# A new order of VectorE's drains and low parts at the beginning of a block, and an earlier split of a22, in a Strassen-style adapter kernel on one core

## The reference, cut to what matters

```python
W = weights[condition]                             # 64 x 64 per batch element, one of 16
c = einsum('bct,bcd->bdt', x, W)                   # x: 64 x 64 x 1024
logits = c_flat @ gate_w.T + expert_bias           # 4 experts
one_hot = one_hot(argmax(logits))
base = einsum('bth,oh->bto', c, W_up)              # W_up: 1024 x 1024
z = einsum('nh,erh->ner', c_flat, lora_A)          # rank 8 for each expert
d = einsum('ner,ehr->neh', z, lora_B)              # ALPHA / RANK is 1
delta = einsum('neh,ne->nh', d, one_hot)           # only the chosen expert's
out = x + base + delta
```

## Time and profile before

| what | value |
|---|---|
| median of three runs | 444.32 us |
| the profiled execution's own time | 443.3 us |
| span of that execution, first to last instruction | 441.4 us |
| TensorE busy | 433.1 us (98%) |
| VectorE busy | 351.6 us (80%) |
| ScalarE busy | 198.3 us (45%) |
| GpSimd busy | 115.9 us (26%) |
| granted TensorE clock over the span | 1.000 |

### The profile page before, as it was taken

How to read it: one execution, slowest core, us unless ns; L and a number is a source line. 1 busy time by engine, 2 the same in 40 slices (tenths; PEclk the granted TensorE clock), 3 DMA queues, 4 the chain that set the end, 5 groups by cost and what they waited for, 6 DMA issues and landing times.

```text
span 441.4 us, 8929 instructions
## 1 busy us (share of the span) xinstructions
PE 433.1 (98%) x3138; PEld 410.5 (93%) x3139; DVE 351.6 (80%) x644; ACT 198.3 (45%) x310; POOL 115.9 (26%) x95
## 2 busy tenths in 40 slices
PE   7999998999999999999999999999999999999997
PEld 7889987999999999999999999999999999999996
DVE  3999879697796969789686969879696977969663
ACT  5895335263444426254543525354352624453210
POOL 3991050220505031040504013050502205050310
PEclk9999999999999999999999999999999999999999
DMA  9900032230403122130313213031222214031102
GB/s 236 404 6 1 1 120 71 75 119 25 162 28 117 50 104 86 48 143 24 119 60 106 71 48 143 24 132 58 95 71 91 99 40 151 24 119 48 73 25 97
DMA packets 17375, 38.73 MB, mean 88 GB/s; under 512 B 3854, under 2 KB 4110, under 8 KB 17362
## 3 DMA queue, kind: packets, MB, share of 16 engines
q1 hardware_dynamic: 16162, 38.02, 24.4%
q10 hardware_dynamic: 1040, 0.26, 0.3%
q0 software_dynamic: 160, 0.28, 0.2%
HBM read 21.78 MB, written 16.78 MB: 87 GB/s over the span
## 4 chain that ended last, share of the span: by engine, by line
PE 86%; DVE 7%; issue 6%; POOL 1%; ACT 0%; DVEq 0%; POOLq 0%
PE bank_y L614 25%; PE bank_x L614 24%; PE y_ps L550 11%; PE bank_c L614 10%; PE bank_b L614 9%; PE bank_x L672 2%; DVE w_s L817 2%; DVE w_a L817 1%; DVE x_hl L784 1%; PE bank_y L620 1%; PE bank_c L620 1%; PE bank_b L620 1%; PE bank_x L620 1%; PE bank_y L651 1%; DVE hl_s L794 1%
## 5 line engine op out<-in xcount | busy, mean ns | idle before, releaser
L326 POOL TENSOR_TENSOR s_sum<-a 128x512 f32<-128x512 f32 x16 | 20.7, 1294 | 294.6 <-DVE a L789 294.6
L384 ACT ACTIVATE x_hl<-x_sb 64x1024 fp32r<-64x1024 f32 x64 | 67.8, 1059 | 57.9 <-DMA x_sb<-in_x_dram 57.1
L784 DVE TENSOR_TENSOR x_hl<-x_sb,x_hl 64x1024 fp32r<-64x1024 f32 x64 | 78.2, 1221 | 8.2 <-ACT x_hl L384 6.2
L614 PE MATMUL bank_x<-w_a,hl_a 128*128 128x292 f32 (+1 forms) x576 | 76.1, 288 | 0.0
L614 PEld LDWEIGHTS bank_x<-w_a,hl_a 128*128 128x128 f32 x576 | 73.5, 189 | 0.5
L614 PE MATMUL bank_y<-w_a,hl_a 128*128 128x256 f32 (+1 forms) x552 | 72.9, 288 | 0.0
L614 PEld LDWEIGHTS bank_y<-w_a,hl_a 128*128 128x128 f32 x552 | 70.7, 189 | 0.4
L388 ACT ACTIVATE y_small<-y_ps 128x512 f32<-128x512 f32 x62 | 37.1, 598 | 74.1 <-PE y_ps L550 74.0
L550 PE MATMUL y_ps<-cond_hl,x_hl 128*128 x496 | 63.7, 271 | 2.3 <-DVE a L789 1.0
L550 PEld LDWEIGHTS y_ps<-cond_hl,x_hl 128*128 128x128 f32 x496 | 61.5, 191 | 4.7 <-DVE a L789 1.5
L789 DVE TENSOR_TENSOR a<-y_ps,y_small 128x512 f32<-128x512 f32 x62 | 42.6, 686 | 12.9 <-ACT y_small L388 12.2
(11 more groups left out here) (129 smaller groups left out, 471.5 us busy)
## 6 DMA issues: line engine op xcount, KB each, us to landing
x_sb<-in_x_dram SPq DMA_DIRECT2D x32, 512.0 KB, 3.3
out_dram<-x_sb SPq DMA_DIRECT2D x63, 256.0 KB, 2.0
w_raw<-in_L_ffn_W_up_dram SPq DMA_DIRECT2D x8, 512.0 KB, 11.3
cond_sb<-in_L_cond_weights_dram ACTq DMA_DIRECT2D x1, 256.0 KB, 5.2
cond_sb<-in_L_cond_weights_dram SPq DMA_DIRECT2D x1, 256.0 KB, 6.2
out_dram<-x_sb SPq DMA_DIRECT2D x2, 128.0 KB, 1.9
router_sb<-in_L_ffn_lora_A_dram POOLq DMA_DIRECT2D x1, 128.0 KB, 7.2
lora_b_sb<-in_L_ffn_lora_B_dram POOLq DMA_DIRECT2D x1, 128.0 KB, 7.9
```

The costliest lines, as they stand in the source:

```text
L326: pool.tensor_tensor(s1_sum[:, :], a21[:, :], a22[:, :], ALU.add).then_inc(s1_added, 1)
L384: act.activation(x_hl[rows, t, b, :], x_sb[rows, 2 * par + t, :], ACT.Copy).then_inc(x_high, 1)
L614: mm = pe.matmul(dst, hl[op][:, a, k, :], w[:, b, k, cols], start=(fresh and k == 0 and a + b == 0), stop=(k == KH - 1 and a == 1), skip_g ...
L784: dve.tensor_tensor(x_hl[other, t, b, :], x_sb[rows, 2 * par + t, :], x_hl[rows, t, b, :].bitcast(fp32), ALU.subtract).then_inc(x_low, 1)
```

## The change

In block q VectorE now drains c21 and c22 of block q-1, writes a22's low part, drains p1, and only then writes the low parts of s2 and s1, in this order (before: c21, low s1, low s2, c22, p1, with a22's low part later, behind `after_p6`). ScalarE rounds a22 first in its block, ahead of s1 and s2, where it did so after s4 and s3. GpSimd, TensorE and SyncE keep their orders. The prologue is untouched. p6 and p5 in the program's names are the products of s2 and s1.

```diff
@@ block.scalar, period
             def period(q, par, closing):
+                round_a22(q, True)
                 round_s1(q, True)
                 round_s2(q, True)
                 if not closing:
                     split_x(q + 1, 1 - par, 0, True)
                 round_s4(q, True)
                 round_s3(q, True)
-                round_a22(q, True)
@@ block.vector, period
                 after_delta21(q - 1, 1 - par)
+                after_delta22(q - 1, 1 - par)
+                low_operand("a22", a22, q)
+                after_p1(q, par)
+                low_operand("s2", s2_sum, q)
                 low_operand("s1", s1_sum, q)
-                low_operand("s2", s2_sum, q)
-                after_delta22(q - 1, 1 - par)
-                after_p1(q, par)
                 if not closing:
                     for b in range(2):
                         split_x(q + 1, 1 - par, 0, b)
@@
                 low_operand("s3", a21, q)
                 after_p6(q, par)
-                low_operand("a22", a22, q)
```

## The result

The changed kernel takes 447.22 us and the kernel before 444.68 us (medians of six executions each, in the same six rounds). The ratio is 1.0057, 95% interval 1.0046 to 1.0069: slower by 2.5 us, 2.0 to 3.1. One execution of each kernel took far longer (939.3 us before, 1492.72 us changed); both are in the medians and neither is in the ratio. The prediction was 446.2 us, +1.9 us, with 444.3 to 448.5 as range.

A forecast was written before the change was run, and what follows sets the result against it. TensorE was taken as the bound, with no slack at `sum_y` of a11: +0.89 - 0.60 = +0.29 us a block, +2.3 us over 13 periods, less 0.4 in block 1, so 444.3 + 1.9 = 446.2 us; range 444.3 to 448.5.

The forecast's parts named there:

- What bounds the kernel: TensorE, busy 98%, has no slack at `sum_y` of a11: each 0.01 us it moves shifts the period by 0.01 us.
- Rival C: Faster if p1 could start on idle VectorE from 115.64, break-even 115.9: sum moves -0.19, time 442.2 us; chance 8%.
- Part 1: VectorE at the block's beginning: p1 starts 0.31 us earlier but low s2 and s1 queue behind it, x 0.89 us later.
- Part 2: VectorE behind p6: a22's low part leaves this place ahead of `sum_y` of a11, saving 0.60 us.
- The sum for a block: `sum_y` of a11 moves +0.29 us; period 25.51 against a mean of 25.33, over 13 periods +2.3 us.
- ScalarE's wait goes: ScalarE's split of x no longer waits for tile t=1's load, since c22 drains 2.4 us earlier; no gain beyond the sum.
- Block 1: Exception entered late from the prologue: TensorE's wait for p1 nearly goes; gain of 0.2 to 1.1 us, taken as 0.4.
- the prediction's later case: In block 1, low s1 waits for GpSimd's s3 and ends near 66.87, so x starts at 66.9 instead of 66.49.
- Rival A: Low s2 runs into GpSimd's s3 and waits 0.18 us a block: 2.3 us more, 448.5 us; chance 12%.
- Rival B: No measurable change: `sum_y` moves 0.15 us less than thought, period 25.36, result 443.6 to 444.3 us; chance 17%.

The follow-up runs named there:

- order-alone run: Kernel before with only VectorE's order at the block's beginning changed (c21, c22, p1, low s2, low s1), a22 left in its old place: 454.24 us, ratio 1.0237.

## Why the prediction was right

- **What bounds the kernel: right, in one direction.** The position of `sum_y` of a11 sets the period. Later by 0.60 (one more low part) it cost 0.50 a block against the mean, 0.61 against block 3. But that each 0.01 us of the sum is 0.01 us of the period was too strong: earlier by 0.29 it gave nothing. (Rival C itself had put TensorE's own pace at 25.20; 25.23 was measured.) Block 3 of before stands just where TensorE's own work takes over. The forecast didn't need the other side of it.
- **Part 1, +0.89 us: right.** 4.39 us became 5.28. VectorE idles 0.52 us for a11's product, 0.5 was said; a22's low part ended 0.54 behind s4's sum, 0.55 was said.
- **Part 2, -0.60 us: right** in the changed kernel, where p6 to x takes 0.72 in place of 1.31.
- **The sum for a block: 25.53 measured, 25.51 predicted**, 2.57 us for 13 blocks where 2.3 were said. With nothing gained in block 1 the profiles account for +2.6 us, and the medians moved by 2.5 in the first session and by 1.9 in the second. That the second equals the predicted 1.9 is luck: its blocks were as long as in the first. The 0.6 us between the sessions is not explained.
- **ScalarE's wait goes: right.** In block 3 its second split of x starts at 7.35 behind delta22 and not 9.35, and no `sum_y` of a11 in blocks 2 to 14 waits for `y_small`.
- **Block 1, -0.4 us: the step that failed**, by its size. It was 0.0 and -0.1 at full clock (28.30 and 28.20 against 28.30) and +0.6 in the profiled execution. Low s1 did wait for s3's sum, and x was split 8.06 us behind delta22, just where the prediction's later case has it (66.9 - 58.84), so the low end of 0.2 was the right one. The rest went where the prediction hadn't looked: ScalarE waited for the load of tile t=1 and split it at 12.51 and not at 12.16, `sum_y` of a11 waited 0.23 us for `y_small`, and so it started 15.47 us behind delta22 where before it started at 15.45. And TensorE's clock could fall.
- **Rival A (low s2 runs into s3)** stayed out by 0.07 us, with 0.08 predicted. The rule of the Trainium skill's page "SBUF — State Buffer" (section "SBUF: two separate sides"), an exclusive lock for the whole instruction, is borne out in kind: the pairs of 3.23 and 3.43 us are waits for whole sums. By its letter, as an estimate, the low part would end its own 0.68 behind s4's sum; it ended 0.54 behind. With the sum of s3 taking 1.29 behind that it would have ended at 118.65, 0.19 after VectorE came to s2, instead of at 118.39. **Rival C (faster)** fell with its condition: p1 starts 0.03 to 0.04 us behind the end of its product, even after 1.97 us of idle time in two runs. Its break-even is off a little: 115.9 is 0.29 ahead of p1's start at 116.18 and 0.24 ahead of the product's end, and against the mean period of 25.33 it would be 116.0. **Rival B** rested on a sum that moves by 0.15 less; it moved by 0.30.

## What to carry to other kernels

In a written-out order, draw the next wait that can't be moved (here the end of a product) and ask which work fits in front of it and which will now queue behind it. What is moved behind it costs its time, less only what the wait begins earlier (1.20 - 0.31 = 0.89 us here), even if the engine idles in front of it. Where two engines hold each other up, an order must also be laid against the other engine's instructions: a start 0.4 us later made the same two low parts 3.43 us long instead of 2.45. And a bound in one direction isn't a bound in the other: one run with the suspect made longer and one with it made shorter tell how much is to be had.

## What the runs showed of the hardware

- A VectorE operation with both operands in SBUF that comes while GpSimd works on SBUF waits for the end of that operation and ends 0.54 to 0.55 us behind it (it takes 0.68 alone); two such in a row against two sums of GpSimd take turns with them (3.23 and 3.43 us for the pair that takes 1.28 alone). Drains, with one operand in PSUM, were not held up (in the order-alone run c22's took 0.68 us from 114.82 on, with s4's sum running from 115.11 and taking its own 1.30).
- TensorE's granted clock fell to a mean of 0.66 of full over 5 us behind two waits of 0.94 and 0.44 us in block 1 in one execution of the changed kernel, and not in two others with the same waits; a product there took 4.59 us in place of 3.01. It fell in the same block in the profiles of three of the variants, behind waits of 0.85 and 0.44, 0.86 and 0.45, and 2.30 us, and not in that of the kernel before, behind 1.22 and 1.04 us.
